# Experts located in twos instead of eights, one counting product per expert, and 72 turns of the identity behind the last logits

## What is computed

```
oh = one_hot(e, 64); pos = cumsum(oh, 0) - 1 at e     # place of a token within its expert
valid = pos < 256
y = einsum(silu(x w_gate[e]) * (x w_up[e]), w_down[e])
out[token] += y_slot * weight                         # scatter-add, sum over the 8 experts of a token
```

## Time and profile before

| | |
|---|---|
| time, 3 runs | 3309.37, 3311.04, 3313.46 us; median 3311.04 |
| the profiled execution's own time | 3304.55 us |
| its span, first to last instruction | 3302.7 us |
| sequence phase | up to 2810.7 us of the span (first DMA issue of the count phase) |
| count phase | 2810.7 to 2839.1 us (end of the last copy) |
| expert phase | 2839.7 us (first GpSimd instruction) to the end |
| busy over the span | TensorE 89%, VectorE 85%, ScalarE 83%, GpSimd 68% |
| mean granted TensorE clock | 0.959 of 2.4 GHz |

### The profile page before, as it was taken

The page is one execution under the profiler, slowest core; times in us unless marked ns, Lnnn a source line. Parts: engine busy times, 40 slices in busy tenths (PEclk is TensorE's granted clock), DMA queues, the critical chain, the costliest instruction groups (busy, mean ns, idle before and its releaser), DMA issues. The chain is left out here.

```text
span 3302.7 us, 55009 instructions
## 1 busy us (share of the span) xinstructions
PE 2943.3 (89%) x18817; PEld 2370.4 (72%) x18817; DVE 2808.4 (85%) x4597; ACT 2730.5 (83%) x5297; POOL 2259.9 (68%) x940
## 2 busy tenths in 40 slices
PE   6999999999999999999999999999999986665664
PEld 4777777777777777777777777777777775544543
DVE  4899999999999999999999999999999997344432
ACT  5999999999999999999999999999999995211110
POOL 1777777677777777676767777776767774377776
PEclk8999999999999999999999999999999998688887
DMA  3112222122222222121112222222222121477774
GB/s 111 58 59 68 70 70 70 58 64 64 70 70 70 70 70 70 61 70 64 62 59 69 70 70 70 70 70 70 70 70 70 51 65 30 118 145 152 148 150 75
DMA packets 196160, 252.80 MB, mean 77 GB/s; under 512 B 45664, under 2 KB 174144, under 8 KB 195904
## 3 DMA queue, kind: packets, MB, share of 16 engines
q1 hardware_dynamic: 171328, 211.73, 20.4%
q0 software_dynamic: 24576, 37.77, 6.9%
HBM read 188.36 MB, written 61.08 MB: 76 GB/s over the span
## 5 line engine op out<-in xcount | busy, mean ns | idle before, releaser
L345 POOL TENSOR_TENSOR hid<-hid,c_all 128x1536 f32<-128x1536 f32 x512 | 1768.4, 3460 | 842.2 <-DVEq L607 821.0
L612 DVE TENSOR_TENSOR_SCAN hid<-decay,hid,psB 128x1024 f32<-128x1024 f32 x512 | 1201.5, 2347 | 82.8 <-PE psB L914 35.2
L386 ACT ACTIVATE decay<-dt,a_neg 128x383 f32<-128x383 f32 x2048 | 1085.8, 604 | 0.5 <-issue 0.2
L914 PE MATMUL psB<-ident,dbu_t 128*128 128x128 f32 x6144 | 852.2, 275 | 87.9 <-DVE hid L612 61.8
L374 ACT ACTIVATE dbu_t<-dtu_t,b_t 128x512 f32<-128x512 f32 x1376 | 893.2, 710 | 4.1 <-PE psB L914 4.0
L914 PEld LDWEIGHTS psB<-ident,dbu_t 128*128 128x128 f32 x6144 | 700.0, 141 | 200.2 <-issue 87.1
L926 PE MATMUL psY<-ident,hid 128*128 128x128 f32 x6144 | 754.3, 273 | 0.1
L926 PEld LDWEIGHTS psY<-ident,hid 128*128 128x128 f32 x6144 | 687.2, 141 | 0.6 <-POOL hid L345 0.4
L612 DVE TENSOR_TENSOR_SCAN hid<-decay,psB 128x512 f32<-128x512 f32 x512 | 623.7, 1218 | 9.6 <-PE psB L914 5.2
L996 PE MATMUL psM<-u,w_dt 128*128 128x384 f32 x1024 | 351.5, 487 | 3.8 <-ACT u L416 3.1
L1407 ACT ACTIVATE e_side<-e_psL,e_in_tile 128x128 f32<-128x128 f32 x128 | 45.8, 363 | 261.9 <-DVE e_in_tile L1531 261.2
(11 more groups left out here) (148 smaller groups left out, 3260.6 us busy)
## 6 DMA issues: line engine op xcount, KB each, us to landing
c_all<-bc_rows_dram SPq DMA_DIRECT2D x128, 768.0 KB, 5.0
out_dram<-h SPq DMA_DIRECT2D x64, 384.0 KB, 5.7
h<-out_dram SPq DMA_DIRECT2D x32, 384.0 KB, 3.5
x_weights_dram<-normed SPq DMA_DIRECT2D x32, 384.0 KB, 2.6
xt<-in_x_t_dram SPq DMA_DIRECT2D x32, 375.0 KB
xs<-in_x_dram SPq DMA_DIRECT2D x32, 256.0 KB
e_wg<-in_gate_dram SPq DMA_DIRECT2D x64, 128.0 KB, 2.8
e_wu<-in_up_dram SPq DMA_DIRECT2D x64, 128.0 KB, 3.0
```

Source lines behind the costliest of these rows:

```text
L345: nc.gpsimd.tensor_tensor(hid[k % 4][:, :, :], hid[k % 4][:, :, :], c_all[:, k, :].unsqueeze(1).to_broadcast([P, CH, L]), ALU.mult).then_i ...
L386: last = nc.scalar.activation(decay[k % 4][:, c, 1:L], dt[q][:, c, 1:L], ACT.Exp, scale=a_neg[:, c, k:k + 1])
L612: nc.vector.tensor_tensor_scan(h[:, lo:hi], flat(decay[k % 4])[:, lo:hi], flat(psB)[:, lo:hi], h[:, lo - 1:lo] if j else 0.0, ALU.mult, AL ...
L914: last = nc.tensor.transpose(flat(psB)[:, i * P:(i + 1) * P], dbu_t[k % 2][:, t, c * P:(c + 1) * P], ident[:, :])
```

## The change

1. Behind the last logits TensorE waits for `s_yz` and turns the identity 72 times into a PSUM tile that nobody reads.
2. The count phase subtracts neighbouring tiles on VectorE first (`steps`, one instruction of 97 x 16 = 1552 elements per group of 16 experts, two buffers), so one product per expert is left. TensorE runs 14 products of the triangle with itself ahead. `total` comes from a second small product with a matrix of distances between tiles (`apart`), beside the one with `prior`; ScalarE and VectorE copy one each. The loops are written out.
3. In the expert phase 6 experts are located ahead instead of 16, and `find_rows` and `stage` work on pairs (`PAIR` = 2), from the first pair on. TensorE's order becomes `turn(e + 1); gather_counts(e + 6); down(e); up(e + 1)`, GpSimd's `scatter(e); gather(e + 4)`. All loops are written out and `s_turn` is gone.

```diff
+            pe.wait_ge(s_yz, NB)
+            for i in range(72):
+                nc.tensor.transpose(psY[:, i % NSEG, 0:P], ident[:, :], ident[:, :])
...
+        step = [sb(f"n_step{q}", [P, NT + 1, NE // CG], BF16) for q in range(2)]
...
+            pe.wait_ge(s_t1, 2)
+            for i in range(14):
+                nc.tensor.matmul(psT[1][:, 0:P + 1], tri[:, 0:P], tri[:, :], start=True, stop=True)
...
+                g = j // (NJ // CG)
                 if j % (NJ // CG) == 0:
-                    pe.wait_ge(s_ld[j // (NJ // CG)], 16)
+                    pe.wait_ge(s_st, g + 1)
                 after(pe, s_uc[q], i)
                 for k in range(UB):
-                    g, e = divmod(j * UB + k, NE // CG)
-                    for d in range(2):
-                        last = nc.tensor.matmul(
-                            psU[q][0:R, k // 2, (k % 2) * (P + 1):(k % 2 + 1) * (P + 1)],
-                            chosen[:, g, 1 - d:1 - d + R, e], tri[:, d, :], start=(d == 0), stop=(d == 1))
+                    e = (j * UB + k) % (NE // CG)
+                    last = nc.tensor.matmul(psU[q][0:R, k // 2, (k % 2) * (P + 1):(k % 2 + 1) * (P + 1)],
+                                            step[g % 2][:, :, e], tri[:, :], start=True, stop=True)
...
+            nc.tensor.matmul(psT[0][0:R, 0:NE], prior[0:R, 0:R], diff[0:R, :, P], start=True,
+                             stop=True).then_inc(s_tp, 1)
+            pe.wait_ge(s_t2, 1)
+            nc.tensor.matmul(psT[1][0:R, 0:NE], apart[0:R, 0:R], diff[0:R, :, P], start=True,
                              stop=True).then_inc(s_tp, 1)
...
+            def steps(g):
+
+                dve.wait_ge(s_ld[g], 16)
+                after(dve, s_u, (g - 1) * (NJ // CG))
+                nc.vector.tensor_tensor(step[g % 2][:, :, :], chosen[:, g, 1:NT + 2, :], chosen[:, g, 0:NT + 1, :],
+                                        ALU.subtract).then_inc(s_st, 1)
+
+            steps(0)
+            steps(1)
+            for i in range(NJ // 2):
                 dve.wait_ge(s_u, 2 * i + 2)
                 nc.vector.tensor_copy(diff_of(2 * i + 1), product(1)).then_inc(s_uc[1], 1)
+                if i in (1, 3):
+                    steps(2 + i // 2)
...
-    STAGED = 6
-    NR = NE // EB
-    LOCATED = 2
+    LOCATED = 6
+    PAIR = 2
...
             for e in range(AHEAD):
-                gather(e, e)
+                gather(e)
             pool.wait_ge(s_zst, 16)
...
+            for e in range(NE):
+                scatter(e)
+                if e + AHEAD < NE:
+                    gather(e + AHEAD)
...
+            for e in range(LOCATED):
+                count(e)
+            silu(0)
+            for e in range(NE):
+                if e + 1 < NE:
+                    silu(e + 1)
+                if e + LOCATED < NE:
+                    count(e + LOCATED)
...
+            for e in range(LOCATED):
+                gather_counts(e)
+            turn(0)
+            up(0)
+            for e in range(NE):
+                if e + 1 < NE:
+                    turn(e + 1)
+                if e + LOCATED < NE:
+                    gather_counts(e + LOCATED)
+                down(e)
+                if e + 1 < NE:
+                    up(e + 1)
...
+            def stage(e):
+                q = e % EB
+                after(dve, s_sc, 16 * NH * (e - EB + 1))
...
+            pass_tiles(0)
+            for e in range(LOCATED):
+                if e + 1 < LOCATED:
+                    pass_tiles(e + 1)
+                enter_tiles(e)
+                if e % PAIR == 1:
+                    find_rows(e // PAIR)
+                    for j in (e - 1, e):
+                        if j < AHEAD:
+                            stage(j)
+            copy_turned(0)
+            for e in range(NE):
+                activate(e)
+                if e + LOCATED < NE:
+                    pass_tiles(e + LOCATED)
+                if e + 1 < NE:
+                    copy_turned(e + 1)
+                scale(e)
+                if e % PAIR == 0 and e + AHEAD < NE:
+                    if e > 0:
+                        find_rows((e + AHEAD) // PAIR)
+                    for j in range(e + AHEAD, e + AHEAD + PAIR):
+                        stage(j)
+                if e + LOCATED < NE:
+                    enter_tiles(e + LOCATED)
```

More of the change, by code:

```diff
@@ L1318, in expert_phase @@
         block = ctx.enter_context(nc.Block())
-        def each(eng, body):
-            for q in range(EB):
-                body(0, q, q)
-            with eng.Fori(1, NR - LOCATED) as i:
-                for q in range(EB):
-                    body(i, EB * i + q, q)
-            for i in range(NR - LOCATED, NR):
-                for q in range(EB):
-                    body(i, EB * i + q, q)
-        def exists(e):
-            return not isinstance(e, int) or e < NE
-        def to_locate(e, q):
-            return e + LOCATED * EB, q % 2
         @block.sync
@@ L1347, in load @@
                 sp.dma_start(wd[q][:, :], w["down"][e]).then_inc(s_wt[q], 16)
-            for q in range(EB):
-                load(q, q)
-            with sp.Fori(1, NE // EB) as i:
-                for q in range(EB):
-                    sp.wait_ge(s_yo, EB * i + q - EB + 1)
-                    sp.sem_inc(s_turn, 1)
-                    load(EB * i + q, q)
             sp.wait_ge(s_zst, 16)
@@ L1365, in _, with gather @@
             nc.gpsimd.iota(slot_i[:, :], pattern=[[P, NH]], base=0, channel_multiplier=1).then_inc(s_io, 1)
-            def gather(e, q):
+            def gather(e):
+                q = e % EB
                 pool.wait_ge(s_st, e + 1)
-                pool.sem_inc(s_turn, 1)
                 for h in range(NH):
@@ L1408, in count @@
                                                 bias=in_tile[p][:, h:h + 1],
[L1409 removed]
+                                                accum_out=place[:, NH * e + h:NH * e + h + 1])
                 last.then_inc(s_pl, 1)
[L1412 to L1421 removed]
+            for e in range(LOCATED):
[6 more added lines that the diff above has]
+                    count(e + LOCATED)
         @block.tensor
@@ L1446, in up, with down @@
                 last.then_inc(s_gu, 1)
-            def down(i, e, q):
-                r = q % 2
+            def down(e):
+                r = e % 2
                 pe.wait_ge(s_at, e + 1)
@@ L1452, in down, with gather_counts @@
                 for h in range(NH):
-                    last = nc.tensor.matmul(psO[r][:, h, :], at[r][:, h * P:(h + 1) * P], wd[q][:, :],
+                    last = nc.tensor.matmul(psO[r][:, h, :], at[r][:, h * P:(h + 1) * P], wd[e % EB][:, :],
                                             start=True, stop=True)
                 last.then_inc(s_yo, 1)
-            def expert(i, e, q):
-                if exists(e + 1):
-                    up(i + (q + 1) // EB, e + 1, (q + 1) % EB)
-                if exists(e + 2):
-                    turn(i + (q + 2) // EB, e + 2, (q + 2) % EB)
-                if exists(to_locate(e, q)[0]):
-                    gather_counts(*to_locate(e, q))
-                down(i, e, q)
-            def gather_counts(e, p):
+            def gather_counts(e):
+                p = e % 2
                 pe.wait_ge(s_ps, e + 1)
```

158 lines of the change are left out of this document (60 added, 98 removed).

## The result

The changed kernel takes **3286.57 us** (median of 4 runs, 3282.39 to 3292.98), the kernel before 3310.43 on the same chip (4 runs, 3309.37 to 3313.46): a ratio of 0.9934 [0.992, 0.9949], 23.9 us less. On a second chip, with many more runs of before (29, median 3305.21), the changed kernel has 3286.35 and a ratio of 0.9948 [0.9931, 0.9965], 18.9 us less. The two profiled executions differ by 3304.55 - 3286.1 = 18.45 us; this is the difference that the profile can explain. The other 5.4 us come from the medians: before's median of 3310.43 lies 5.9 us above its profiled execution, the changed kernel's 0.5 above its own.

A forecast was written before the change was run, and what follows sets the result against it. TensorE was taken to bound the count phase and GpSimd's 6.59 us per expert the expert phase; 4.75 + 7.2 - 0.7 + 1.0 = 12.25 us off the median 3311.04 gave 3298.8 us, range 3289 to 3305.5.

The forecast's parts named there:

- Turns: Identity transposes behind the last logits: clock rises after 4.7 us, TensorE done 0.7 us too late for the next load.
- the first rival: Transposes behind the logits never raise the clock, everything behind starts 5.9 us late: 3304.0 us, chance 0.08.
- Counting at 1.2 GHz: Count phase: its matmuls will hardly hold a raised clock, so they were priced at 0.182 us each.
- the counting keeps 2.4 GHz: Count phase holds the clock raised by the transposes, 3 us more saved, fast subtraction maybe 1.6: 3294.5 us, chance 0.22.
- the term of 4.75 us: Count phase saving: 7.7 from halved matmuls, less 1.9 and 0.9 for subtractions and 0.15 for the second total product.
- +1.9 us: Count phase, before the first product: the first subtraction at 1.77 us, with its hand-overs, lies on the path.
- 16.6 + 0.9 us of stalls: Count phase: eight rounds of one buffer take 16.6 us; the third and fourth subtractions add 0.45 each.
- the term of 7.2 us: Expert phase start: first scatter 7.2 us earlier, through earlier first gather and `up`, then 8.9 us from `up` to scatter.
- Early periods, 1.0 us: First scatter periods of the expert phase: 1.0 us of the first period's excess goes, ends 0 to 3.
- Steady state, 0: Later expert phase: GpSimd keeps the pace at 6.59 us per expert, no change, between -3 and +5.
- the slow rival: Expert phase: TensorE's chain of `up` behind `down` sets the pace, 7.7 us per expert at 1.2 GHz: 3365 us, chance 0.05.
- the fast-clock rival: Same as the counting keeps 2.4 GHz: count phase at the raised clock, 3294.5 us, chance 0.22.

The follow-up runs named there:

- experiment 2: Only the new count phase put into the kernel before, the rest as before: median 3299.82 us, ratio 0.9985.
- experiment 5: The changed kernel without the 72 turns of the identity and their wait: median 3283.49 us, ratio 0.9933.
- experiment 6: The changed kernel without the 14 products ahead of the counting: median 3282.02 us, ratio 0.9929.
- experiment 4: The kernel before with all hardware loops written out and the s_turn increments gone: median 3310.34 us, ratio 1.0015.
- experiment 10: The changed kernel with three PSUM buffers instead of two in the counting: median 3279.79 us, ratio 0.995.
- experiment 12: The changed kernel without turns and 14 products, three PSUM buffers, rows found in twos for experts 0 to 15, then eights: median 3276.5 us, ratio 0.9932.
- Experiment 8: The changed kernel with 16 experts located ahead and rows found by eights, indices staged one expert at a time: median 3288.17 us, ratio 0.9953.
- experiment 7: The changed kernel with TensorE's old order in the expert phase and VectorE's copies moved to match: median 3298.37 us, ratio 0.9968.
- experiment 11: The changed kernel with TensorE's old order and GpSimd's gather ahead of the scatter again: median 3290.19 us, ratio 0.9971.
- experiment 3: Only the new expert phase put into the kernel before, counting and logits as before: median 3296.0 us, ratio 0.997.

## Why the prediction was right in direction and too small

**Turns.** Forecast 0.7 us late, measured 0.12 and 0.26: transposes alone raised the clock after 4.3 us (forecast 4.7), so the first rival is out. The Trainium skill (TensorE: Matmul & The Clock Gate, Part 4: PE-mode transpose) says that transposes do not engage the fast clock; for these float32 ones the measurement decides against it. My price of a slow turn was a little low: by its own rows (1.49 - 0.4)/5 is 0.218 us, not 0.213.

**Counting at 1.2 GHz.** Right: 0.50 through all of it. The rival "the counting keeps 2.4 GHz" did not occur, and with it went the only use that I saw in the turns and the 14 products; experiments 2, 5 and 6 show no other. Whether the products fail to keep the clock or the idle time in front of them loses it is open (experiment 6).

**Counting, the term of 4.75 us: the step that failed first.** It was 7.9. By its steps:
- From load to first product I had +1.9 us; it was 4.24 against 3.37, +0.87. Of the difference, 0.8 is the subtraction: 0.97 us, not the 1.77 that I drew from the slope of float32 operations. The near end, 0.96, was the right one. The Trainium skill (VectorE: DVE Perf Modes, the perf-mode tier table) gives bfloat16 operands twice the float32 rate, and this trace agrees with it: 1552 elements in 0.97 us. I had priced a bfloat16 operation by a float32 slope.
- From first product to the end of the last copy I had 16.6 + 0.9 us of stalls; it was 15.25 us (24.33 before). The way round the buffer is 1.78 us instead of 2.0, 1.5 us in seven rounds: 0.09 instead of 0.23 to VectorE's copy, because that copy no longer runs in a hardware loop (experiment 4 shows 0.14 less for the loops alone), and 0.05 instead of my estimate of 0.14 back. With the short subtraction, the third and fourth fit into VectorE's pauses: another 0.9.
- From the last copy to the expert phase I had +0.15; it was 1.61 against 1.27, +0.34.
- That the ring of two buffers is the bound is shown by experiments 10 and 12: a third buffer takes 2.3 to 2.7 us off this stretch.

**Start, the term of 7.2 us: the second that was mis-sized.** It was 8.4. First gather 5.6 us earlier (forecast 4.9), first `up` 5.96 earlier (6.0, and the reason given for it, VectorE locating six instead of sixteen, fits). The rest failed in size: from `up` to scatter 7.66 us, not 8.9. `down` ran at clock 1.00 in 1.08 us, and between the Silu and `down` stood 0.97 us, not the 1.5 of product, weight column, compare and counts in a row. Experiment 8 splits the term: locating in twos 28.1 - 21.9 = 6.2 us, the orders 30.3 - 28.1 = 2.2. But the two help each other: once experts are located in twos, TensorE's order alone is worth 26.7 - 21.9 = 4.8 us (experiment 7).

**Early periods, 1.0 us.** The first period lost 1.24 us, as said, and the first eight 3.7 (57.34 before, 53.61 after). In the first profile the later periods gave 2.4 us of it back: 10 of them were over 6.9, eight of these ended by the scaling or by a landing scatter. In the second they did not. The two pairs together say 3.1 us (420.5 to 417.4), the top of my 0 to 3. But the first periods vary with the start in front of them: in experiments 2 and 4, with the old orders, the start is 2 us longer and the first eight periods 54.65 and 55.06 us. The sum of start and first eight periods is steadier: 86.7 to 88.4 us in the four profiles with the old orders and sixteen located, 74.9 to 77.1 in the six with the changed expert phase. That is some 12 us, where I had 7.2 + 1.0; the later 55 periods have 362.3 to 365.2 and 358.4 to 366.4 us and show no difference.

**Steady state, 0.** The number held, and part of the reason did not. I called GpSimd's new order (scatter first) free, because a gather keeps three periods to its expert. With TensorE's old order it isn't: `turn(e + 2)` in front of `down(e)` needs rows whose gather has only just gone out, and in experiment 7 scatters wait 12.9 us for the scaling. The size is uncertain: by the profile of experiment 7 some 12 us against the mean of the six, by the times of experiments 7 and 11 about 3. So TensorE's new order is not only a quicker start, as I had it; it also takes this wait away. I also read the earlier trace rows wrongly: of the idle time in front of the scatters only 1.0 us ends with a landing scatter, 29.2 us with nothing that the profile shows. The sum of the period does not hang on it. That the slow rival (TensorE's ring at 7.7 us) did not occur is in the mean clock of 0.84 from 2920 to 3180 us and in 6.6 us per period.

**The range.** By its terms the forecast should have been 7.9 + 8.4 + 1 to 3 - 0.2 = 17 to 19 us. So the mechanism was right, and what failed are sizes: the counting by 3.1 us (the subtraction's price and the way round the buffer), the start of the expert phase by 1.2, and by about 4 with its first eight periods. My range gave the fast subtraction to the fast-clock rival only, though it could happen alone and did; and its own sum, 3298.8 - 3.0 - 1.6 - 4, is 3290.2, not 3289. Yet 17 to 19 us off 3311.04 are 3292 to 3294, inside the range. That the time came out below it took the other 5 us as well, by which four executions of before lay above its profiled one; in 29 runs on another chip they were not there. That part is chance, and no term of mine stood for it.

## What to carry to other kernels

Price an operation by a row of its own data type, and if there is none, let both ends into the range. When two engines' orders change together, ask of each whether it is free only because of the other: here scatter-first shows no cost with TensorE's new order and makes scatters wait with the old one. Before a difference between two profiles is called a cost, see where each profiled execution stands among its kernel's runs: the 13 us between experiments 7 and 11 are a slowest against a fastest one, and the times don't show them. A warm-up of TensorE is worth nothing until the trace shows that the work behind it keeps the clock.

## What the runs showed of the hardware that I had not expected

- The granted clock stayed at 1.00 for 4.2 us of idling (experiment 6) and then was 0.50 in a stretch where TensorE was busy 13.95 of 14.90 us. Products with 97 columns of weights and 129 of data, one each 0.18 us, never raised the clock, 64 or 128 of them, in any of the fourteen profiles; 72 dense transposes did, after 4.3 us.
- Executions of one kernel differ in the sequence phase alone: the last logits ended between 2788.5 and 2806.7 us in fourteen profiles whose code up to there is the same but for its last turns. Hence a single profile can't price a change of 10 us by its span. Behind the landmark the parts repeat better: the stretch of the counting within 0.6 us (21.10, 21.02, 20.54, 20.78, 20.81 and 20.95 us) but for two profiles at 21.57, the start of the changed expert phase from 21.45 to 21.97 us, and 22.57 in experiment 3. The 63 periods differ by 8 us with one and the same expert phase.
- A hardware loop on the copying engine, with an address that comes from its counter, adds 0.1 to 0.14 us to the hand-over from TensorE (the first copies of experiment 4 against three profiles in loops).
- ScalarE and VectorE can stop together for 1 to 2 us with no engine of the core named at the end of it (experiments 2 and 4).
